# GpSimd's eight row scatters of a sequence issued as two groups of four

## The reference, cut to what matters

```python
x = x + layernorm(attention(layernorm(x)))      # gated linear attention, 16 heads of 64, 4 key heads
x = x + layernorm(moe(layernorm(x)))            # 8 experts of width 512, each token uses 2

# attention, per head and step:   S = exp(g_t)[:, None] * S + k_t (outer) v_t ;  o_t = q_t @ S
# moe:  logits = x @ router_w.T + router_b ; top 2 ; gates = softmax(top 2)
#       out += gate_e * ((silu(x @ gate_e.T) * (x @ up_e.T)) @ down_e.T)
```

## Time and profile before

| what | value |
|---|---|
| time of three runs | 1336.64, 1340.28, 1340.60 us (median 1340.28) |
| the profiled execution's own time | 1339.43 us |
| its span (first to last instruction of the trace) | 1337.6 us |
| TensorE busy | 1195.0 us, 89% of the span |
| VectorE busy | 771.7 us, 58% |
| ScalarE busy | 641.0 us, 48% |
| GpSimd busy | 551.7 us, 41% |
| mean granted TensorE clock | 0.961 of full speed |

### The profile page before, as it was taken

One profiled execution on the slowest core, in us unless ns is written; L12 is line 12 of the kernel. 1 busy time (PEld: TensorE's weight loads), 2 busy tenths in 40 slices (PEclk: granted clock), 3 DMA queues, 4 the chain that ended last, 5 costly groups with the idle time before them and its releaser, 6 DMA issues.

```text
span 1337.6 us, 29226 instructions
## 1 busy us (share of the span) xinstructions
PE 1195.0 (89%) x8910; PEld 962.3 (72%) x8910; DVE 771.7 (58%) x2380; ACT 641.0 (48%) x1653; POOL 551.7 (41%) x686
## 2 busy tenths in 40 slices
PE   7998988989889898898998988948999999999895
PEld 4876857658577585675766857737899998998872
DVE  5676766767667676676676766752333333333327
ACT  3753646437355374463643646323444444443336
POOL 2244354444544445435444454242333333333226
PEclk9998999999999999999999999968999999999998
DMA  6001010010100101101001010033311111111335
GB/s 258 9 25 33 8 39 16 24 32 12 35 19 21 32 18 30 32 8 35 18 26 32 8 32 16 21 135 102 111 47 49 47 48 47 47 47 47 107 139 207
DMA packets 59675, 67.49 MB, mean 50 GB/s; under 512 B 6896, under 2 KB 49664, under 8 KB 59264
## 3 DMA queue, kind: packets, MB, share of 16 engines
q1 hardware_dynamic: 48720, 41.10, 9.8%
q0 software_dynamic: 8448, 17.45, 4.0%
q10 hardware_dynamic: 2480, 8.61, 1.9%
HBM read 37.98 MB, written 29.15 MB: 50 GB/s over the span
## 4 chain that ended last, share of the span: by engine, by line
PE 72%; DVE 11%; issue 9%; ACT 4%; DMA 3%; POOL 1%; DVEq 0%; another core or an unknown queue 0%; POOLq 0%; ACTq 0%; SPq 0%
PE pO L761 9%; PE pO L594 8%; PE pO L599 6%; PE pW L627 5%; PE pA L578 5%; PE pA L752 4%; PE pA L753 4%; PE pA L552 4%; PE pJ L753 4%; PE pJ L752 4%; PE pT L610 3%; PE pO L563 3%; DVE qT L1113 2%; PE pJ L627 2%; PE pJ L512 2%
## 5 line engine op out<-in xcount | busy, mean ns | idle before, releaser
L1605 POOL DMA_INDIRECT expert_out<-y,tail x136 | 130.6, 960 | 263.8 <-ACT y L1020 236.6
L871 ACT ACTIVATE sq<-pO 128x512 f32<-128x512 f32 x128 | 75.9, 593 | 252.1 <-PE pO L594 203.9
L594 PE MATMUL pO<-vJ,aT 128*128 128x128 f32 x1024 | 140.8, 280 | 14.0 <-DVE aT L1150 14.0
L594 PEld LDWEIGHTS pO<-vJ,aT 128*128 128x128 f32 x1024 | 125.5, 191 | 35.0 <-issue 32.2
L1537 POOL DMA_INDIRECT expert_rows<-x1n,rowi x120 | 117.5, 979 | 63.5 <-issue 43.8
L761 PE MATMUL pO<-wdown_sb,vJ 128*128 128x128 f32 x1088 | 134.4, 277 | 0.0
L1157 DVE TENSOR_REDUCE ss<-sq 128x8 f32<-128x512 f32 x128 | 87.0, 679 | 78.1 <-ACT sq L871 76.5
L761 PEld LDWEIGHTS pO<-wdown_sb,vJ 128*128 128x128 f32 x1088 | 128.5, 194 | 0.0
L1405 DVE TENSOR_TENSOR vJ<-pA,kJ 128x256 f32<-128x256 f32 x136 | 57.5, 425 | 109.1 <-ACT kJ L1009 108.7
L599 PE MATMUL pO<-S_mid,qT 128*128 128x128 f32 x896 | 118.3, 275 | 0.0
L599 PEld LDWEIGHTS pO<-S_mid,qT 128*128 128x128 f32 x896 | 109.1, 192 | 0.0
(11 more groups left out here) (234 smaller groups left out, 2442.5 us busy)
## 6 DMA issues: line engine op xcount, KB each, us to landing
xt<-expert_rows SPq DMA_DIRECT2D x69, 130.0 KB
xa<-x SPq DMA_DIRECT2D x16, 256.0 KB, 2.7
xr<-x SPq DMA_DIRECT2D x16, 256.0 KB, 2.9
after_attention<-x SPq DMA_DIRECT2D x16, 256.0 KB
arena<-after_attention ACTq DMA_DIRECT2D x8, 512.0 KB
expert_rows<-zeros SPq DMA_DIRECT2D x8, 390.0 KB
expert_out<-y,tail POOLq DMA_INDIRECT x136
wgate_sb<-wgate SPq DMA_DIRECT2D x1, 2048.0 KB, 9.8
```

Source lines behind the costliest of these rows:

```text
L594: last = mm(o[:, g, h, :, :], aT[:, c % 2, h, g * P:(g + 1) * P], vJ[:, c, h, :], start=(h == 0 and g == 0), stop=(c == 0), skip_group_che ...
L1605: g.indirect_dma_start(out=ys_dram, in_=y[:, k, :], in_offset=None, out_offset=bass.IndirectOffsetOnAxis(ap=tail[:, k, 1:2].bitcast(U32), ...
```

## The change

The function `scatter` is cut in two: `ready_to_scatter` holds its waits, and `scatter` issues a single DMA. In a turn the scatters of tiles 0 and 1 stay where all eight were. Those of tiles 2 and 3 stand behind `mids`, as the last of the turn. The wait for all scatters of a sequence moves from the end of its turn to the next turn, behind `norm_apply` and ahead of `router_norm`. Turn 1 leaves the loop, since no scatters lie behind it: the loop on GpSimd is `Fori(2, S - 1)`. In turn 15, which has no `mids`, the second four follow the first at once. The order of the eight scatters among themselves is the same, and the other engines' code is untouched.

```diff
-            def scatter(i):
+            def ready_to_scatter(i):
                 pool.wait_ge(tail_ready, i * 2 + 2)
                 settle(pool)
                 pool.wait_ge(rowi_ready, i + 1)
                 settle(pool)
-                for t in range(NT):
-                    for k in range(2):
-                        g.indirect_dma_start(out=xs_dram, in_=x1n[:, k, t, :], in_offset=None,
-                                             out_offset=bass.IndirectOffsetOnAxis(ap=rowi[:, k, t:t + 1], axis=0))\
-                            .then_inc(scattered, 16)
+
+            def scatter(t, k):
+                g.indirect_dma_start(out=xs_dram, in_=x1n[:, k, t, :], in_offset=None,
+                                     out_offset=bass.IndirectOffsetOnAxis(ap=rowi[:, k, t:t + 1], axis=0))\
+                    .then_inc(scattered, 16)
...
                 if routed:
+                    if not at_start(i - 1):
+                        scattered_all(i - 2)
                     router_norm(i - 1)
                     copy_rows(i - 1)
...
                 if routed:
-                    scatter(i - 1)
+                    ready_to_scatter(i - 1)
+                    for t in range(2):
+                        for n in range(2):
+                            scatter(t, n)
                 if more:
                     residual(i, 2)
...
-            with pool.Fori(1, S - 1) as i:
+
+            def turn_and_mids(i):
                 turn(i, True, True)
                 mids(i + 1, i)
-                scattered_all(i - 1)
+                for t in range(2, NT):
+                    for n in range(2):
+                        scatter(t, n)
+
+            turn_and_mids(1)
+            with pool.Fori(2, S - 1) as i:
+                turn_and_mids(i)
             turn(S - 1, True, False)
+            for t in range(2, NT):
+                for n in range(2):
+                    scatter(t, n)
```

## The result

The changed kernel takes 1260.07 us (median, 1256.39 to 1261.36) against 1339.22 us for the kernel before in the same session (1336.64 to 1340.60): a ratio of 0.941, 95% interval 0.938 to 0.943. The forecast was 1258 us. The profiled execution took 1258.83 us, for which the sum had given 1257.4.

What follows compares the result with a forecast made beforehand. TensorE's chain was taken to be held up at L563 by long runs of scatters. 1339.4 - 86.2 + 14 x (0.1 + 0.2) = 1257.4 us, forecast as 1258 us, range 1250 to 1272.

Steps and rivals of the forecast that it cites:

- the first term: L563 to the scores: with scatters 5 to 8 gone, 15.43 us falls to 9.25; 86.2 us saved in all.
- The pause left at L563's start: TensorE at L563: leftover pause after the first four scatters, between nothing and one 1.43 us step; 0.1 us a turn taken.
- The tail of 1.50 us: TensorE at L563: pauses go on 1.50 us after the eighth scatter; the same was assumed behind the fourth.
- GpSimd late by 0.2 us a turn: GpSimd around `norm_apply`: loop branch and moved wait together cost 0 to 0.98 us a turn, taken as 0.2.
- The two charged items: Costs set against the saving: 0.1 us at L563's start and 0.2 us for GpSimd's branch and wait, in 14 turns.
- Partial pauses: Rival at L563 and the turn's head: each group of four still leaves pauses, 2.86 us a turn; 1297 us, chance 0.15.
- Loop code: Rival at L563: the pauses belong to TensorE's code in the loop, not to scatters; 1341 us, chance 0.10.
- Slower: Rival at the next turn's head: the hold-up moves with the second four scatters, 9.0 us lost; 1381 us, chance 0.09.

## Why the prediction was right

**The place and the cause.** The prediction put the 48.6 us at L563 and the 52.0 us at L1176 down to the eight scatters. The split without the move (1337.86 us) and the busy GpSimd without scatters (1259.94 us) show that it is the scatters' place, and not the edit's other parts or GpSimd's work as such. The prediction took for granted that the hold-up is part of the program; on three of the four chips of the experiments it isn't there, and the first term would be worth nothing. The profile that it read came from a chip that has the hold-up, and so did the result; that is what made the number right.

**The first term.** Forecast: 86.2 us from the way L563 to scores. Measured: 87.8. It was a little low because the place came out at 9.14 us a turn and not at the 9.25 of the undisturbed turn 0, which is 14 x 0.11 = 1.5 us.

**The pause left at L563's start, 0.1 us a turn.** Measured: none. The first four end 1.2 us before the run (362.95 - 361.77), and it is whole. The tail of 1.50 us, which the prediction put behind the fourth scatter too, was not seen there.

**GpSimd late by 0.2 us a turn.** Measured: no lateness that anyone pays. The four start 0.15 us behind the last state, not 0.49, and so end at 12.94 us after L563's start (375.89 - 362.95), not at 13.48; branch and wait passed in that slack. L1461 starts 0.37 us after `rstd` (376.41), where 0.39 had been the undisturbed distance.

**What the sum did not have.** The late mask signal (13 x 0.26 = 3.4 us) and three drops of the clock (3 x 1.3 = 3.9), 7.2 us as read, in place of the 4.2 us charged. 1339.4 - 87.8 + 7.2 = 1258.8, which is what the execution took. The two charged items were wrong in kind, and what came in their place was 3.0 us more; the first term gave 1.6 us more than forecast. That the sum is off by only 1.4 us is luck. The turns with a lower clock are not the moved scatters' doing: the kernel before has them too on a chip without the hold-up (last section), though not where its turns are held up.

**The rivals.** Partial pauses (1297 us): not seen; the 0.26 us is its small remainder. Loop code (1341 us): refuted, since the same loop runs L563 whole after the move, and in the kernel before on other chips. Slower (1381 us): its mechanism is real, as all eight behind the states showed, with the masks late by up to 5.9 us; it took eight scatters there, not four. The point from which it decides, 6.1 us lost a turn, was reached by the eight (the rest of the turn is 46.3 us in the mean there, 7.0 more than the 39.3 before, with GpSimd's lateness in it) and by far not by the four (0.26 us). The reason given against it, that signals are not late under the first four or five scatters, does not hold in general: with four over the run one came 4 us late.

**The rule that spoke against it.** The Trainium skill, "SBUF — State Buffer", section "Who interferes with whom", has it that DMA traffic and compute engines don't contend. On the first chip DMAs from GpSimd delayed what TensorE announces by 4 us and more, which the rule does not cover; the traces of the three others show nothing against it.

**What stays open.** Why one chip has the hold-up and three have not; nothing in the program or in the scatters' durations differs, and only the missing landing times mark it in the traces. What resource is shared between the scatters and TensorE's signals: the trace shows that signals come late and that TensorE then stops, not what they queue for. Whether their descriptors or their packets do it. And how many scatters, how close to which matmuls, are harmless on a chip with the hold-up: under the first two of the eight a signal came on time, under the first of four beside the dense run it did not. Scatters spread over the states or put under the query projections never ran on such a chip.

## What to carry to other kernels

An engine that stops inside a run of its own instructions ("issue") or waits for a releaser without a name may be held up by a signal that is under way: look for what else is in flight at that time, and for a turn of the same loop in which it isn't; the difference between the two, turn by turn, is the gain to expect. On a chip with the hold-up, scatters that GpSimd starts are best kept away from a dense run of small matmuls and from the hand-overs right behind it: four over the run made the way from it to the scores about 13.0 us long, in place of 9.14, while four at the head of the turn cost 0.26. Eight in a row cost 6 to 7 us a turn at either place. And before a gain of some per cent is believed, run both kernels on more than one chip: this change is worth 6% where the hold-up is and nothing where it isn't.

## What the runs showed that I had not expected

- The same program, before: 1337.69 us on one chip and 1256.23, 1255.67 and 1255.12 us on three others. The hold-up costs the kernel 6% and the change takes nearly all of it away (1260.07 against 1256.01 for the changed kernel on a chip without it).
- Where it is present, VectorE waits up to 5.9 us for the announcement of work that TensorE has finished, and ScalarE waits with it (up to 5.5 us). TensorE itself was seen to stop only in the run of 56, and in 28 turns of two runs the first pause came 6.73 to 6.80 us after the first scatter.
- With all eight scatters at the head of the turn the kernel takes the time that it takes with all eight at L563 (1336.64 and 1337.69 us), though part of it may be GpSimd's own lateness.
- The traces taken where the hold-up is present give no landing time for the scatters, the others 2.3 or 2.4 us.
- The granted clock drops without the hold-up too: in the kernel before on the third chip, four of fourteen turns take 49.98 or 49.99 us, the others 48.42 to 48.66.
